# Two-layer cross-attention: the low part of each batch's fourth block subtracted on DVE, two weight loads and one weight product at other places

## The reference

```python
def _L0_xattn_ref(q_feat, kv_feat, ...):
    qn = _layer_norm(q_feat, g_q, be_q)
    kvn = _layer_norm(kv_feat, g_kv, be_kv)
    q, k, v = qn @ Wq.T + bq, kvn @ Wk.T + bk, kvn @ Wv.T + bv
    attn = jax.nn.softmax(jnp.einsum('bne,bme->bnm', q, k), axis=-1)
    ctx = jnp.einsum('bnm,bme->bne', attn, v)
    return q_feat + (jnp.einsum('bne,fe->bnf', ctx, Wd) + bd)

def _L1_xattn_ref(img_embed, sent_embed, atten_mask, Wq, Wk, Wv, Wo, gamma, beta):
    H, D = 8, 256
    Q = (img_embed @ Wq).reshape(B, -1, H, D).transpose(0, 2, 1, 3)
    K = (sent_embed @ Wk).reshape(B, -1, H, D).transpose(0, 2, 1, 3)
    V = (sent_embed @ Wv).reshape(B, -1, H, D).transpose(0, 2, 1, 3)
    score = jnp.einsum('bhqd,bhkd->bhqk', Q, K) / math.sqrt(D)
    score = jnp.where(mask, score, -jnp.inf)
    attn = jax.nn.softmax(score, axis=-1)
    ctx = jnp.einsum('bhqk,bhkd->bqhd', attn, V).reshape(B, -1, H * D)
    out = ctx @ Wo + img_embed
    mu = jnp.mean(out, axis=-1, keepdims=True)
    var = jnp.var(out, axis=-1, keepdims=True)
    return (out - mu) * jax.lax.rsqrt(var + EPS) * gamma + beta
```

## Time and profile before

| | us |
|---|---|
| median of 3 timed runs | 522.11 (522.06 to 522.51) |
| the profiled execution | 522.48 |
| its span, first to last instruction | 520.7 |
| PE busy / DVE busy / ACT busy / GpSimd busy | 481.5 / 333.5 / 289.9 / 241.7 |

### The profile page before, as it was taken

How to read it: one execution, slowest core, us unless ns; L and a number is a source line. 1 busy time by engine, 2 the same in 40 slices (tenths; PEclk the granted TensorE clock), 3 DMA queues, 4 the chain that set the end, 5 groups by cost and what they waited for, 6 DMA issues and landing times.

```text
span 520.7 us, 7533 instructions
## 1 busy us (share of the span) xinstructions
PE 481.5 (92%) x2424; PEld 398.7 (77%) x2424; DVE 333.5 (64%) x681; ACT 289.9 (56%) x465; POOL 241.7 (46%) x136
## 2 busy tenths in 40 slices
PE   1989999999959999999999999999999999999992
PEld 1867787767748887888788878888888788778892
DVE  5999774666365657565756575657565755675357
ACT  4676575567364655565555556556565655557222
POOL 4646565455634363635362637171726263353004
PEclk9999999999969999999999999999999999999997
DMA  8313023856744664566456644665475646561002
GB/s 268 126 42 121 1 61 126 244 161 217 235 136 157 194 208 164 193 202 203 156 174 201 200 163 161 202 201 177 145 236 176 200 137 217 174 191 42 0 2 81
DMA packets 53974, 81.97 MB, mean 157 GB/s; under 512 B 5792, under 2 KB 43072, under 8 KB 53824
## 3 DMA queue, kind: packets, MB, share of 16 engines
q1 hardware_dynamic: 44992, 50.16, 33.7%
q10 hardware_dynamic: 8960, 31.54, 15.6%
HBM read 49.16 MB, written 32.51 MB: 157 GB/s over the span
## 4 chain that ended last, share of the span: by engine, by line
PE 59%; DVE 13%; ACT 9%; DMA 8%; issue 7%; POOL 1%; SPq 1%; ACTq 1%; DVEq 0%; POOLq 0%
PE ps_scores L594 20%; PE ps_o L616 5%; PE ps_o L618 4%; PE ps_o L620 4%; PE ps_o L619 4%; PE ps_o L617 4%; DVE probs L1310 4%; DMA probs_t_lo<-scratch 3%; DMA scratch<-probs 3%; ACT probs L952 2%; ACT o_hi L990 2%; DVE o_lo L1328 2%; PE ps_task L542 2%; PE ps_task L544 2%; PE ps_task L543 2%
## 5 line engine op out<-in xcount | busy, mean ns | idle before, releaser
L489 POOL TENSOR_TENSOR probs_t_lo<-probs_t_lo,probs_t_hi 128x1024 fp32r<-128x1024 f32 x60 | 144.0, 2400 | 193.6 <-ACT probs_t_hi L962 193.5
L962 ACT ACTIVATE probs_t_hi<-probs_t_lo 128x1024 fp32r<-128x1024 f32 x60 | 63.1, 1052 | 34.5 <-DMA probs_t_lo<-scratch 34.2
L616 PE MATMUL ps_o<-probs_t_hi,val_hi 128*128 128x512 f32 (+1 forms) x144 | 58.7, 407 | 7.6 <-DVE o_lo L1328 7.4
L618 PE MATMUL ps_o<-probs_t_hi,val_lo 128*128 128x512 f32 (+1 forms) x144 | 57.0, 396 | 0.0
L619 PE MATMUL ps_o<-probs_t_hi,val_rem 128*128 128x512 f32 (+1 forms) x144 | 56.9, 395 | 0.0
L620 PE MATMUL ps_o<-probs_t_lo,val_rem 128*128 128x512 f32 (+1 forms) x144 | 56.9, 395 | 0.0
L617 PE MATMUL ps_o<-probs_t_lo,val_hi 128*128 128x512 f32 (+1 forms) x144 | 56.8, 395 | 0.0
L1273 DVE RECIPROCAL row_inv<-row_sum 128x1 f32<-128x1 f32 x72 | 11.2, 157 | 70.4 <-PE ps_scores L594 68.7
L1310 DVE STREAM_TRANSPOSE probs<-probs 128x1024 f32<-128x1024 f32 x30 | 37.3, 1245 | 24.9 <-ACT probs L952 24.9
L594 PE MATMUL ps_scores<-key_hi,q_hi 128*128 128x512 f32 x144 | 46.6, 405 | 2.9 <-DVE neg_scores L1286 1.7
L1310 DVE STREAM_TRANSPOSE neg_scores<-neg_scores 128x1024 f32<-128x1024 f32 x30 | 37.2, 1241 | 14.3 <-ACT neg_scores L952 14.3
(11 more groups left out here) (247 smaller groups left out, 1105.0 us busy)
## 6 DMA issues: line engine op xcount, KB each, us to landing
probs_t_lo<-scratch SPq DMA_DIRECT2D x240, 128.0 KB, 3.0
scratch<-neg_scores ACTq DMA_DIRECT2D x30, 512.0 KB, 3.2
scratch<-probs ACTq DMA_DIRECT2D x30, 512.0 KB, 3.6
ring<-in_weights_a SPq DMA_DIRECT2D x9, 512.0 KB, 5.9
ring<-in_weights_b SPq DMA_DIRECT2D x9, 512.0 KB, 5.1
ring<-in_keys_t SPq DMA_DIRECT2D x4, 512.0 KB, 3.1
ctx_raw<-in_context SPq DMA_DIRECT2D x2, 768.0 KB, 9.0
ring<-in_context SPq DMA_DIRECT2D x16, 96.0 KB, 2.7
```

Of the source, the lines that this page charges most:

```text
L489: nc.gpsimd.tensor_tensor(pt_lo[b][:, t, :, :], pt_lo[b][:, t, :, :].bitcast(f32), pt_hi[b][:, t, :, :].bitcast(f32), ALU.subtract).then_i ...
L616: pe.matmul(o0, val_hi[b][:, kt, :], hi, start=first, stop=False)
L618: pe.matmul(o0, val_lo[b][:, kt, :], hi, start=False, stop=end)
L962: act.activation(pt_hi[b][:, t, :, :], pt_lo[b][:, t, :, :].bitcast(f32), ACT.Copy)\
```

## The change

- The subtraction for the fourth block of each batch is made by DVE, in a new function `split_last`, which adds to a new semaphore `last_split`; `split_moved` on GpSimd returns at once for these blocks (15 of 60). In the heads 1 to 7 `split_last(h, 0)` stands ahead of the minimum of j = 5, and `split_last(h - 1, 1)` ahead of that of j = 1. In head 1, j = 1, and in head 0, j = 5, it stands behind the minimum. The first part of `values` waits for three blocks on `moved_split` and for the fourth on `last_split`.
- `load_a(1)` is issued ahead of `fetch(0, 4)`. `load_b(h)` is issued behind `fetch(h, 0)`, or in head 1 behind `fetch(1, 1)`.
- In head 0, PE makes `absorb(0, 6)` in step 5, ahead of `scores(0, 6)`.
- In head 0, ACT issues `spill(0, 7)` ahead of `round_moved(0, 5)`.

```diff
@@ def body(h), SP @@
                     if h == 0 and j == 4:
                         values(PC_V11, 1, 1)
+                        load_a(1)
                     fetch(h, j)
                     if h == 0 and j == 0:
                         load_b(0)
-                    if (j == 4 if h else j == 5) and h < HEADS - 2:
+                    if 0 < h < HEADS - 2 and j == 4:
                         load_a(h + 1)
-                    if j == 7:
-                        load_b(h + 1)
+                    if j == (1 if h == 1 else 0) and h > 0:
+                        load_b(h)
@@ def split_moved(h, j), GpSimd @@
-                r, b = slots1(h, j), j // QT
+                b = j // QT
+                if j % QT == QT - 1:
+                    return
                 t = slice(4 * (j % QT), 4 * (j % QT) + 4)
-                pool.wait_ge(moved_hi, r + 1)
+                pool.wait_ge(moved_hi, slots1(h, j) + 1)
@@ def values(h, b, c), PE @@
-                        pe.wait_ge(moved_split, 8 * h + QT * (b + 1))
+                        pe.wait_ge(moved_split, 6 * h + 3 * (b + 1))
+                        pe.wait_ge(last_split, 2 * h + (b + 1))
@@ def first_body(), PE @@
                     if j == 5:
                         folded_queries(task_no(0, 5), 0)
+                        pe.wait_ge(piece_split, pieces_b(0))
+                        pe.wait_ge(task_free, task_no(0, 5))
+                        absorb(task_no(0, 6), 0)
+                    if j == 7:
+                        pe.wait_ge(task_free, task_no(0, 7))
+                        absorb(task_no(0, 7), 1)
                     if j >= 6:
-                        if j == 6:
-                            pe.wait_ge(piece_split, pieces_b(0))
-                        pe.wait_ge(task_free, task_no(0, j))
-                        absorb(task_no(0, j), j - 6)
                         values(0, 0, j - 6)
@@ def first_body(), ACT @@
+                    if j == 7:
+                        spill(0, 7)
                     if j == 2 or j >= 6:
                         round_moved(0, j - 2)
-                    if j != 1:
+                    if j != 1 and j < 7:
                         spill(0, j)
@@ DVE @@
+            def split_last(h, b):
+
+                t = slice(4 * (QT - 1), 4 * QT)
+                dve.wait_ge(moved_hi, 8 * h + QT * (b + 1))
+                dve.tensor_tensor(pt_lo[b][:, t, :, :], pt_lo[b][:, t, :, :].bitcast(f32),
+                                  pt_hi[b][:, t, :, :].bitcast(f32), ALU.subtract).then_inc(last_split, 1)
@@ def first_body(), DVE @@
                     if j == 5:
+                        split_last(0, 0)
                         split_task(0, j)
@@ def body(h), DVE @@
                 for j in range(2 * QT):
+                    early = not (known and h == 1 and j == 1)
+                    if early and j == 1:
+                        split_last(h - 1, 1)
+                    if j == 5:
+                        split_last(h, 0)
                     minimum(h, j, 1)
+                    if not early:
+                        split_last(h - 1, 1)
```

More of the change, by code:

```diff
@@ L286, in build @@
         moved_split = sem("moved_split")
+        last_split = sem("last_split")
         valued = sem("valued")
```

## The result

| | median, us | runs | ratio to before, 95% interval |
|---|---|---|---|
| before | 522.31 | 4 | |
| changed | 540.71 (536.95 to 543.37) | 4 | 1.0345 (1.0306 to 1.0384) |

The change costs 18.4 us where 5.4 were predicted; the time lies outside the predicted range. Its mean granted clock is 0.985; that of the others is 0.986, 0.980 and 0.979.

The account below looks back on a forecast made before the run. It took TensorE's work plus its gaps to bound the kernel. Loop and last head +13.1, junction -4.9 and clock -2.85 gave +5.35, so 527.5 us against the median of 522.11; range 522.2 to 532.0.

Parts of the forecast that it names:

- The loop's delay: DVE's subtraction ahead of the minimum: 6.7 us at j = 5, 5.2 at j = 1, 1.2 in last head; 13.1 lost.
- The hold by GpSimd at j = 1: GpSimd's third-block subtraction holds up DVE's; minimum 1.0 us late in each of six heads, 0.5 without it.
- Nothing in the change touches a transfer around it: Loop, j = 5: the fetch that sets the fourth block's rounding keeps its time; 7.52 us from spill to rounding.
- The clock: Where heads 0 and 1 meet: with one gap of about 2.1 us the clock stays up, 2.85 us won.
- rival (a): The clock falls again where heads 0 and 1 meet, 2.85 us not won, 530.3 us; chance 0.22.
- The junction: Heads 0 to 1: block (0, 7) rounded at 138.5, value product at 145.7 in place of 150.61; 4.9 us won.
- GpSimd's relief and the transfers at the junction: 15 subtractions of 2.4 us off GpSimd: 0; `load_a(1)` ahead of `fetch(0, 4)`: 0, with 1 us as bound.
- The last head: At j = 5 the minimum comes 1.9 us late; with about 0.75 us of cover, 1.2 us lost.

Follow-up runs that it names:

- both cures: Changed kernel with the loop's weight loads issued between the two waits of a batch's first fetch, and unread matmuls in TensorE's `o_lo` waits: 531.93 us, ratio 1.0179.
- the moves with the junction filled: Changed kernel with GpSimd subtracting all blocks again, plus 10 unread matmuls in the wait where heads 0 and 1 meet: 518.17 us, ratio 0.9917.

## Why the prediction was wrong

Direction, mechanism and the largest term held; two steps around them failed, and a third was half right. The difference of 13.2 us (540.7 against 527.5) splits by the runs into +4.3 for load and spill, +4.5 for the clock in the loop, +3.6 for the junction and +0.7 for the loop's own delay. These are differences of successive kernels, so it is no check that their sum of 13.1 comes near; how it divides between the clock and the rest is sure to 1 or 2 us only, as said above. The rows for the first point are from the second profile of the changed kernel: shortest, median and longest of the 15 instructions of L1325, and the longest with its neighbour on GpSimd:

```profile
L1325 DVE TENSOR_TENSOR probs_t_lo<-probs_t_lo,probs_t_hi x15: 1224/1226/1541, 119.3 to 485.8; 128x1024 fp32r<-128x1024 f32 x15
```

```profile
298.78 2.41 POOL L493 TENSOR_TENSOR probs_t_lo<-probs_t_lo,probs_t_hi 128x1024 fp32r<-128x1024 f32 x1 [1.65 <-ACT probs_t_hi L969]
...
300.73 1.54 DVE L1325 TENSOR_TENSOR probs_t_lo<-probs_t_lo,probs_t_hi 128x1024 fp32r<-128x1024 f32 x1 [1.26 <-ACT probs_t_hi L969]
```

- **The loop's delay, 13.1 us predicted, 13.8 measured** (both cures against the moves with the junction filled). Right in sum; the parts are not as even as the sum. In the profiles of these two the half head that ends with the product of step 6 is 1.0 to 1.2 us longer in four of six heads, as costed (1.12), but 1.4 in head 1 and 2.7 in head 2. The one that ends at step 2 is 0.64 to 0.85 us longer and not 1.0, with 1.2 in the last head. That the total is so near is in part luck.
- **The hold by GpSimd at j = 1** exists, and is 0.3 us at most in the changed kernel, not 0.5. In all seven held places of its two profiles DVE's subtraction ends 1.07 to 1.09 us after GpSimd's, where it takes 1.22 by itself. So GpSimd keeps it up to the end, as the rule of the Trainium skill says that was cited (SBUF — State Buffer, "Who interferes with whom"). What I had too large was the price of the overlap, by about 0.14 us, and I counted it in every head; in the first profile three of 15 places are held, in the second four.
- **"Nothing in the change touches a transfer around it": the step that failed.** The change issued no transfer elsewhere at j = 5, but it delayed the spill against `load_a`: by 0.76 us where the margin was 1.06, and wherever the fourth block was late besides, as in head 1 from the start, the spill fell behind the load. I had kept 7.52 us from spill to rounding; it was 7.8 to 8.3 in the slow course. 4.3 us (536.21 to 531.93).
- **The clock: the second step that failed.** The prediction looked for it at the junction alone and took 2.85 us as won. It fell there too (rival (a)), though for 3.4 us and not 10.2, and it fell again behind waits of 1.6 to 2.3 us in the loop, where I had made 12 such waits and given them no clock. 4.5 us by the medians (536.21 against 540.71), 3.6 with the later runs of the changed kernel.
- **The junction: half right.** The first profile has the predicted times (139.02, 146.23), and 7.2 us from rounding to product was exact. But the other profiles with all moves and `o_hi` in its old place have the product at 147.5 to 148.4: `spill(0, 7)` comes at 132.1 to 132.7 and not at 130.65, and from it to the rounding pass 8.0 to 9.2 us and not 7.5 to 7.8. The first profile is the earliest of the eight; that it met the prediction was luck. The moves are worth 4.2 us where 4.9 + 2.85 were in the sum.
- **GpSimd's relief and the transfers at the junction, both 0:** no run takes them apart. As before the change, no wait for GpSimd's `probs_t_lo` is in the list of the changed kernel. Block (0, 4), behind the moved `load_a(1)`, is rounded 9.4 us after its spill and not 8.9, but `spill(0, 6)` isn't later for it (126.10 and 126.18). That the earlier weight product alone gives nothing was right; with the loads moved, it and the spill may give 1.0 (by ratios) to 1.6 us (by medians).
- **The last head, 1.2 us:** from the product of step 2 to the end, 66.8 us in the changed kernel and 64.6 before, 2.3 more; with both cures 65.5 against 64.5.

**Open:** the two profiled executions of the changed kernel (536.95 and 535.36) are the fastest of their groups of runs. Of the other four, 539.14 to 543.37 us, three have a mean clock of 0.979 or 0.980, lower than the 0.985 and 0.987 of the profiled ones; how many heads they spent in the slow course no profile shows. Nor was it found why the fourth block lands late in step 1 of the last head in nearly every kernel (waits of 1.8 to 3.0 us with the subtraction on DVE ahead of the minimum, `o_hi` in its old place and nothing filled in, 0.9 to 1.2 without the subtraction there).

## To carry to other kernels

When an edit delays one instruction, look not only at who waits for it but at what now passes it on another queue: a transfer that was a microsecond behind another can come ahead of it, and in a loop that can hold itself. Repeated waits of TensorE are to be priced with a share of clock as well as at their length; here it fell behind some waits from 1.64 us up, and not behind all. Before work is moved to an engine on the chain, look for an instruction on the chain that stands behind a wait it doesn't need; here its move was worth 7 us.

## What the runs showed that I had not expected

- A hardware loop whose instructions are the same each time ran in two courses within one execution, 1.0 and 1.5 to 2.3 us of wait for each product, and changed over in head 4 in one profile and behind step 5 of head 2 in the other.
- A wait of TensorE of 1.64 us was followed by 3.4 us at 1.2 GHz, one of 2.07 us by none; with the waits filled by unread matmuls the clock stayed up.
- Taking away waits of 0.2 to 0.35 us, 0.56 us in each head, gave 1.1 us in each head.
